# First expert tile turned inside the last projection, the last three gate tiles moved into the first up products

## What is computed

```python
x = x + xattn(layernorm(x), ctx, mask, Wq, Wk, Wv, Wo, bo)
h = layernorm(x)
scores = sigmoid(h @ gate.T + bias)                 # 9 experts
top, selected = top_k(scores, 2); top = top / (sum(top) + 1e-20)
for e in range(9):
    out += cw[:, e:e+1] * ((silu(h @ w1[e].T) * (h @ w3[e].T)) @ w2[e].T)
x = x + out
```

## Time and profile before

| | before |
|---|---|
| median of three runs | 441.45 us (439.77 to 442.72) |
| the profiled execution | 439.8 us, its span 438.0 us |
| TensorE busy | 408.5 us (93%) |
| VectorE, ScalarE, GpSimd busy | 294.6, 233.4, 253.1 us |
| mean granted clock of TensorE | 0.984 |

### The profile page before, as it was taken

One profiled execution on the slowest core, in us unless ns is written; L12 is line 12 of the kernel. 1 busy time (PEld: TensorE's weight loads), 2 busy tenths in 40 slices (PEclk: granted clock), 3 DMA queues, 4 the chain that ended last, 5 costly groups with the idle time before them and its releaser, 6 DMA issues.

```text
span 438.0 us, 10047 instructions
## 1 busy us (share of the span) xinstructions
PE 408.5 (93%) x3133; PEld 308.6 (70%) x3133; DVE 294.6 (67%) x719; ACT 233.4 (53%) x407; POOL 253.1 (58%) x187
## 2 busy tenths in 40 slices
PE   8799899999999999677999999999999999999981
PEld 8577577777777787564676777777777777777760
DVE  1868898999999999988879765444444444444320
ACT  3556697888788833406754443444444444444430
POOL 4504799998898974324126554555555555555242
PEclk9999999999999999988999999999999999999996
DMA  8963246766766425117886987999888899888782
GB/s 268 366 245 103 75 133 185 197 192 168 198 186 201 151 70 194 36 49 208 189 153 131 167 140 132 143 139 141 142 140 140 127 144 148 139 138 140 115 103 25
DMA packets 107408, 66.38 MB, mean 152 GB/s; under 512 B 82400, under 2 KB 100704, under 8 KB 107360
## 3 DMA queue, kind: packets, MB, share of 16 engines
q1 hardware_dynamic: 99680, 55.25, 54.1%
q0 software_dynamic: 7680, 10.49, 16.1%
HBM read 36.23 MB, written 9.96 MB: 105 GB/s over the span
## 4 chain that ended last, share of the span: by engine, by line
PE 75%; DVE 13%; DMA 3%; ACT 3%; issue 3%; POOLq 0%; DVEq 0%; POOL 0%; SPq 0%; ACTq 0%
PE ps L744 28%; PE ps L757 14%; PE ps L596 11%; PE ps L573 10%; PE ps L584 3%; PE ps L495 2%; PE ps L568 2%; DMA work<-work 2%; PE ps L534 1%; DVE w_all L1014 1%; DVE work L1059 1%; PE ps L542 1%; DVE work L1068 1%; DMA stage<-in_wt 1%; DMA work<-xn_rows,idx_all 1%
## 5 line engine op out<-in xcount | busy, mean ns | idle before, releaser
L744 PE MATMUL ps<-w_all,work 128*128 x960 | 151.6, 315 | 1.0 <-DVE w_all L1117 0.6
L744 PEld LDWEIGHTS ps<-w_all,work 128*128 128x128 f16 x960 | 94.1, 99 | 48.9 <-issue 1.7
L1546 POOL DMA_INDIRECT out_rows<-work,idx_all x40 | 63.3, 1584 | 94.4 <-ACT work L940 84.5
L1386 DVE SCALAR_TENSOR_TENSOR work<-ps,work 128x352 f32<-128x352 f32 x80 | 41.4, 523 | 67.9 <-PE ps L744 65.9
L757 PE MATMUL ps<-w_all,work 128*128 x680 | 80.8, 273 | 2.6 <-DMA work<-work 2.6
L757 PEld LDWEIGHTS ps<-w_all,work 128*128 128x128 f16 x680 | 66.1, 98 | 13.8 <-issue 3.5
L1525 POOL DMA_INDIRECT work<-xn_rows,idx_all x40 | 54.1, 1351 | 32.7 <-DVE work L1379 11.8
L1473 POOL TENSOR_TENSOR w_all<-stage,w_all 128x1088 f16<-128x1088 f32 x28 | 63.1, 2253 | 13.8 <-ACT w_all L827 13.8
L935 ACT ACTIVATE work<-work 128x704 f16<-128x704 f32 x40 | 31.6, 789 | 61.7 <-DVE work L1386 59.8
L929 ACT ACTIVATE work<-ps 128x352 f32<-128x352 f32 x80 | 36.2, 461 | 43.1 <-PE ps L744 42.6
L573 PE MATMUL ps<-w_all 128*128 128x462 f16 (+1 forms) x288 | 57.4, 336 | 0.0
(11 more groups left out here) (146 smaller groups left out, 542.7 us busy)
## 6 DMA issues: line engine op xcount, KB each, us to landing
stage<-in_wt SPq DMA_DIRECT2D x36, 544.0 KB, 4.4
work<-in_x SPq DMA_DIRECT2D x30, 128.0 KB, 3.7
out_rows<-work SPq DMA_DIRECT2D x18, 128.0 KB, 4.5
xn_rows<-work SPq DMA_DIRECT2D x18, 128.0 KB, 4.2
w_all<-in_x SPq DMA_DIRECT2D x1, 1536.0 KB, 14.2
work<-work SPq DMA_TRANSPOSE x79
w_all<-in_wk SPq DMA_DIRECT2D x2, 512.0 KB, 5.1
w_all<-in_wq SPq DMA_DIRECT2D x4, 256.0 KB, 6.7
```

The lines of the kernel that those rows point to most:

```text
L744: mm = pe.matmul(ps[:, c, 0:half], xt[:, t % 2, block, :], weights(wbase + off, half), start=(k == 0 and n == 0), stop=(k == KD - 1 and n ...
L1386: dve.scalar_tensor_tensor(out=sg[:, t % 2, cols], in0=ps[:, 2 + c, 0:HID // 2], scalar=1.0 / SP_W, in1=sg[:, t % 2, cols], op0=ALU.mult, ...
L1546: pool.indirect_dma_start(out=acc, out_offset=bass.IndirectOffsetOnAxis(ap=idx_all[:, t:t + 1], axis=0), in_=yb[:, t % 2], in_offset=None, ...
```

## The change

On **TensorE** the first expert tile is turned inside the last projection, ahead of chunk 7 (`X0_AT`). Only `gate_turn(13)` stays ahead of up(0); the logits of tiles 13, 14 and 15 go into the middle of up(0), up(1) and up(2), and `gate_turn(14)` and `gate_turn(15)` behind up(0) and up(1). The first expert id is read ahead of the last projection. On **ScalarE** the sigmoids come in two parts, for token tiles 0 to 10 in the drain and 11 to 15 at tile 3, and a one-element Silu stands ahead of `first_high`; so a table of functions is loaded at these places and again ahead of silu(4). On **VectorE** `first_low` comes ahead of the picks of tiles 11 and 12 and of w_rest(28); the residual and the normalisation of the last tiles go behind `fx_low(1)`, the logits of tile 13 behind w_rest(31), those of 14 and 15 into tiles 1 and 2. `shares` works on 11 tiles at tile 1 and on 5 at tile 5. **GpSimd** issues gather(2) ahead of `rstd(15)`, and **SyncE** turns tile 1's tokens ahead of two row stores.

```diff
-            def project(i):
+            def project(i, midway=None):
...
+                    if c == X0_AT and midway:
+                        midway()
...
                 warm(WARM_OUT, WARM_LATE)
-                project(NT - 1)
-                first_turn()
+                eids[0] = expert(0)
+                project(NT - 1, first_turn)
                 gate_turn(NT - 3)
-                gate_logits(NT - 3)
-                gate_turn(NT - 2)
-                gate_logits(NT - 2)
...
-            def next_expert(t):
-                if t < NF:
-                    eids[t] = expert(t)
+            def between(s):
+                if s < 3:
+                    gate_logits(NT - 3 + s)
+                if s + 1 < NF:
+                    eids[s + 1] = expert(s + 1)
...
-                if s == 0:
-                    gate_turn(NT - 1)
-                    gate_logits(NT - 1)
+                if s < 2:
+                    gate_turn(NT - 2 + s)
...
             gate_copy(NT + 1 - LAG_G)
+            sigmoids(0, K1)
             w_direct(4 * EARLY + 1)
+            w_direct(4 * EARLY + 2)
+            act.activation(mx[:, 0, 0:1], eps[:], ACT.Silu)
             first_high()
-            gate_copy(NT - 3)
-            w_direct(4 * EARLY + 2)
...
+                if n == 0:
+                    silu(n)
                 if onf(n, -2) and n > -2:
                     fx_high(n + 2)
                 if n == -1:
-                    gate_copy(NT - 2)
+                    gate_copy(NT - 3)
                     w_direct(4 * EARLY + 3)
...
-                if n == 1:
-                    sigmoids()
-                if onf(n, 0):
+                if onf(n, 0) and n > 0:
                     silu(n)
-                if n == 0:
-                    gate_copy(NT - 1)
+                if n in (0, 1):
+                    gate_copy(NT - 2 + n)
                 if n == 3:
+                    sigmoids(K1, NT)
...
                 held_of(0)
-                pick(NT - LAG_G)
                 normalise2(NT - 3)
                 logits(NT + 1 - LAG_G)
+                first_low()
+                pick(NT - LAG_G)
                 pick(NT + 1 - LAG_G)
                 w_rest(4 * EARLY)
-                residual(NT - 1)
-                first_low()
-                stats(NT - 1)
-                aggregate(NT - 1)
-                normalise2(NT - 2)
-                logits(NT - 3)
-                pick(NT - 3)
-                w_rest(4 * EARLY + 1)
...
                 if n == -1:
+                    residual(NT - 1)
+                    stats(NT - 1)
+                    aggregate(NT - 1)
+                    normalise2(NT - 2)
+                    w_rest(4 * EARLY + 1)
                     w_rest(4 * EARLY + 2)
                     normalise2(NT - 1)
-                    logits(NT - 2)
+                    w_rest(4 * EARLY + 3)
+                    logits(NT - 3)
+                    pick(NT - 3)
+                if n in (1, 2):
+                    logits(NT - 3 + n)
+                if n == 1:
                     pick(NT - 2)
-                    w_rest(4 * EARLY + 3)
...
                 if n == 2:
+                    pick(NT - 1)
+                    experts_of(1)
                     w_rest(4 * E9 - 4)
...
                 if n == 5:
+                    shares(1)
```

More of the change, by code:

```diff
@@ L344, in build @@
         WARM_BANK, WARM_LATE = 5, 2
+        X0_AT = 7
         B_CUTS = (0, 4, NCH)
@@ L448, in _ @@
             load_w(4 * EARLY + 3)
-            store_x1(NT - 1)
-            store_xn2(NT - 2)
             def turn_hidden(t):
@@ L475, in fstep @@
                 if n == -1:
+                    store_x1(NT - 1)
+                    store_xn2(NT - 2)
                     store_xn2(NT - 1)
@@ L692, in first_turn, with expert @@
                 mm.then_inc(x0_mm, 1)
+            def expert(t):
+                pe.wait_ge(eid_ok, 1 if t < NF1 else 2)
+                return pe.value_load(eid[0:1, t:t + 1], min_val=0, max_val=E9 - 1)
+            eids = {}
             def drain():
@@ L728, in weights, with up @@
                 return w_all[:, bass.ds(off, n)]
-            def up(t, wbase, after_gates):
+            def up(t, wbase, midway):
                 if t == 0:
@@ L747, in up @@
                     if c == 1:
-                        after_gates()
+                        midway()
             def down(t, wbase):
@@ L780, in _ @@
                         pe.wait_ge(w_lo_ok, 4 * E9)
-                    up(s, eids[s] * (2 * WC), lambda: next_expert(s + 1))
-                if s == 0:
-                    gate_turn(NT - 1)
-                    gate_logits(NT - 1)
+                    up(s, eids[s] * (2 * WC), lambda: between(s))
+                if s < 2:
+                    gate_turn(NT - 2 + s)
                 if s == 2:
@@ L853, in gate_copy, with sigmoids @@
                 act.activation(xn2t, ps[:, 7, 0:D].rearrange("p (k t) -> p k t", k=KD), ACT.Copy).then_inc(xn2t_ok, 1)
-            def sigmoids():
-                act.wait_ge(top_ok, NT)
-                act.activation(R["sgm"], top_val[:, 0:2 * NT].rearrange("p (i k) -> p k i", k=2), ACT.Sigmoid).then_inc(sig_ok, 1)
+            def sigmoids(i0, i1):
+                act.wait_ge(top_ok, i1)
+                act.activation(R["sgm"][:, :, i0:i1], top_val[:, 2 * i0:2 * i1].rearrange("p (i k) -> p k i", k=2),
+                               ACT.Sigmoid).then_inc(sig_ok, 1)
             def step(n):
@@ L1223, in held_of, with shares @@
                 dve.tensor_scalar(held[:, lo + 1:lo + n], r["ef"][:, 0:n - 1], 16.0, None, ALU.mult).then_inc(held_ok, 1)
[L1225 to L1234, removed]
+            def shares(ph):
+                lo, hi = (0, K1) if ph == 0 else (K1, NT)
+                sgm, cwv, v1, v2 = (a[:, :, lo:hi] for a in (r["sgm"], r["cwv"], r["val"][:, 0], r["val"][:, 1]))
+                wsum, wrec = r["wsum"][:, lo:hi], r["wrec"][:, lo:hi]
+                dve.wait_ge(sig_ok, ph + 1)
+                link(dve.tensor_tensor(wsum, sgm[:, 0], sgm[:, 1], ALU.add))
+                link(dve.tensor_scalar(wsum, wsum, 1e-20, None, ALU.add))
+                link(dve.reciprocal(wrec, wsum))
+                link(dve.tensor_tensor(cwv, sgm, wrec.unsqueeze(1).to_broadcast([P, 2, hi - lo]), ALU.mult))
+                link(dve.tensor_copy(v1, cwv))
+                link(dve.tensor_tensor(v2, cwv, v1, ALU.subtract))
             def tile_weights(ph):
@@ L1371, in first_shares @@
             def first_shares():
-                shares()
+                shares(0)
                 link(tile_value(r["u1"][:, :, :, 1, :], ueq1, 1, K1, NF1))
@@ L1412, in fstep @@
                     hidden(n)
-                if n == 0:
-                    logits(NT - 1)
-                    pick(NT - 1)
-                    experts_of(1)
                 if n == 1:
@@ L1563, in fstep @@
                     rstd(NT - 2)
-                    rstd(NT - 1)
                 if onf(n, -3):
                     gather(n + 3)
+                if n == -1:
+                    rstd(NT - 1)
             for n in range(F_FIRST, F_LAST):
```

## The result

The changed kernel takes 444.95 us (median of 4 runs, 444.55 to 446.68) beside 440.61 us (439.21 to 442.72) for the kernel before: ratio 1.009, interval 1.0056 to 1.0125. Its profiled execution has a span of 442.7 us against 438.0. The forecast of 442.8 had the sign and the places, but only a third of the size: +1.4 us was forecast, +4.3 came by the medians and +4.7 by the spans.

What follows compares the result with a forecast made beforehand. TensorE, busy 93% of the span, and its holes bound the kernel. +1.0 us at first_weights and +0.4 from silu(4) make +1.4: span 439.4, 441.2 like the profiled execution, forecast 442.8 from the median; range 440.0 to 446.0.

Steps and rivals of the forecast that it cites:

- the forecast's own mechanism: The forecast's chain of shifts at up(1), first_weights and up(5), together +1.4 us; chance 0.52, expected at 441.3 to 444.5.
- Start of up(0): TensorE behind the last projection: up(0) starts at about 197.4, 3.9 us earlier, and is over at 201.45.
- The new wait: TensorE ahead of gate_turn(14): stands 4.85 us for logits(13), behind w_rest(31) and its later load.
- Rival A: At gate_turn(14): logits(13) come in time and the front gain is kept; 437.7, or 436.5 without clock loss; chance 0.09.
- The clock: TensorE's clock falls again after the empty 4.85 us, now in up(1), costing 1.4 us, between nothing and 1.7.
- Rival B: Clock also falls ahead of up(5), 1.7 us more; load(31) up to 3.0 slower; both from 445.9 up; chance 0.13.
- Rival D: A wash: clock holds in up(1), only logits(15) delays first_weights, by 0.5 us; 442.0 or 441.5; chance 0.22.
- Start of up(1): On TensorE, up(1) starts at 206.55 instead of 207.87, 1.3 us earlier.
- the wait for logits(15): Ahead of first_weights: logits(15), moved to tile 2 on VectorE, end at 216.5; the wait adds 0.3 us.
- The table load: ScalarE, right ahead of silu(4): a 1.28 us load makes up(5) wait 1.1; down(4)'s old wait gives 0.7 back.
- rival C: On ScalarE: switching tables costs a drain on top of the load; 444.2 us; chance 0.04.
- shares(1): VectorE at tile 5: six small instructions, 1.4 us at most, covered by 1.9 us spare between h_low(5) and down(5).

Runs made afterwards that it cites:

- x10: The changed kernel itself, unchanged, timed and profiled a second time: ratio 1.0111 to the kernel before.
- x5: The changed kernel with w_rest(28) ahead of first_low on VectorE again: ratio 0.9998 to the kernel before.
- x6: The changed kernel with w_rest(28) ahead of first_low and the logits and pick of tile 13 ahead of w_rest(29): ratio 1.0018 to the kernel before.
- x3: The changed kernel with 70 matmuls on constants between up(0) and gate_turn(14): ratio 1.0118 to the kernel before.
- x4: The changed kernel with the logits and pick of tile 13 ahead of w_rest(29) to w_rest(31) on VectorE: ratio 1.0071 to the kernel before.
- x2: The changed kernel with a one-element Silu ahead of w_direct(35), loading the table in ScalarE's idle time: ratio 1.0077 to the kernel before.
- x8: x7 with w_rest(31) moved behind hidden(0) on VectorE: ratio 1.0036 to the kernel before.
- x9: x7 with fx_low(2) directly behind w_rest(29), and one load and turn_tokens(2) ahead of the last row store: 439.71 us, ratio 0.9959 to the kernel before.
- x1: The changed kernel with the second part of the shares at tile 6 instead of tile 5: ratio 1.0070 to the kernel before.
- x7: The changed kernel with the edits of x1, x2 and x6, and the picks of tiles 11 and 12 ahead of first_low: ratio 0.9973 to the kernel before.

## Why the prediction was right, and where it was off

**The range.** 444.95 lies within 440.0 to 446.0, but 0.45 above the 441.3 to 444.5 that were given for the forecast's own mechanism. And the median of before came out at 440.61, 0.84 below the 441.45 that 442.8 was built on: the miss in the difference, 2.9 us by the medians, shows as 2.15 in the time. That part of the hit is luck, and the terms below are measured as shifts.

**Start of up(0): right.** 197.4 forecast, 197.74 found; it is over at 201.85 (201.45). The projection with the turn inside ended 0.3 us later than assumed; reading the id ahead made the wait before the projection 0.27 us longer (it starts at 192.29, not 192.10; TensorE reads the id from 191.3 to 192.1, when p_low is there already, at 191.89). It had been costed at nothing.

**The new wait: right in mechanism, and in size in this execution.** 4.85 us forecast, 4.89 found, both ends 0.4 us later, over the chain as written, down to the load at 4.0 us. In the second profile (x10) the load took 5.1 and the hole was 6.0, so the exact match is partly luck. One thing was seen too lightly. The forecast named the load as what is late, at 0.5 us behind VectorE's other work. x5 shows that with the load early 2.9 us of hole remain: the logits were late by their place in VectorE's order anyway. Rival A, the logits in time, would have needed both edits at once, and x6 has them: up(1) at 203.75, 6.25 us after up(0), where A had 203.7 by the transposed tokens. So A had the next bound right, but not the end: it gave 437.7, and x6 is level with before, since up(2), up(5) and down(5) wait next. (The 436.5 beside it has no working.)

**The clock: right that it falls, wrong in size.** "It falls again, now in up(1), and costs 1.4 us, between nothing and the 1.7": up(1) took 6.66, 1.2 more than the forecast 5.45, and 2.7 more than the 3.95 of x3. The upper bound was a single case taken for a limit. Over seven such holes, in six kernels, from 2.9 to 6.0 us long, the cost was 1.1 to 2.7; 1.4 lay inside, 1.7 did not bound it. Of the missed 3.3 us, 1.2 is this term in the profiled execution. x10 lost only 1.7 there, so most of this part belongs to the execution, not to the kernel. Rival B expected a second fall at up(5), which came in no run, and a slower load(31), which came in part: 5.1 us in x4 and x10. Rival D had the clock hold; of the kernels with the hole at the gate turn only x3, with the hole filled, shows that, and its median gained nothing.

**Start of up(1): -0.68 for -1.3.** Logits and gate turn were some 0.4 us later than forecast (206.74 for 206.3), and the gate turn took 0.45 at the low clock where 0.25 was taken: 0.6 us. With the clock's 1.2 they are the 1.8 us by which up(2) missed its forecast (+2.03 for +0.2).

**first_weights: the wait for logits(15) was small.** Forecast +0.3 for it. The logits are over at 218.15 and first_weights starts at 218.21; up(2) took 4.14 us, where up(1) in x3, with nothing to wait for, took 3.95. So some 0.2 us of wait are left. The forecast had 4.05 for up(2) and 0.3 for the wait, 0.2 too much together.

**The table load: right.** Start of the load to the next ACTIVATE 1.29 us again (231.64, 232.93), TensorE's hole 1.13 for 1.1, and x2 takes it away. No drain beside it, the next instruction follows 0.01 us behind the load: rival C falls. The 0.64 us that down(4) waited before was given back, as forecast.

**shares(1): the step that failed.** "The spare 1.9 covers it" took 4.0 us for the transpose, from the earlier trace rows, which is that of the tile before. The transpose of tile 5 is this row of the chain of waits after:

```profile
243.97 5.62 DMA work<-work
```

5.62 us. SyncE's row of its issue in before is

```profile
239.43 1.31 SPq L456 DMA_TRANSPOSE work<-work  x1
```

and down(5) started at 245.18, 5.75 later, without a hole. If the transpose took as long there as after, nothing was spare, and not 1.9. How long it did take in before no row shows, only that it had landed within those 5.75 us. But tile 5's transpose was slower than tile 4's in every profile that shows it as a wait: 5.0 to 5.9 us (the change twice, x2 to x6), where tile 4's took 4.0 to 4.1 (before, x2, x8, x9). The price with the cover gone was given (1.4, found 1.5), and the cover was gone. This is 1.6 of the missed 3.3 us (from down(4) to down(5) 7.16 us, and 6.81 in x10, where before had 5.57), and x1 takes it back. So the trace of before held no proof of the slack: the 5.75 us leave some 1.8 spare only if this transpose, too, takes 4.0.

Together 1.2 for the clock, 0.6 for the start of up(1), 1.6 for shares, less 0.2 ahead of first_weights: 3.2 of 3.3.

What stays open: whether load(35) in x3 was slow by chance, why tile 5's transpose takes longer than tile 4's, and why a transpose of tile 1's tokens took at most 4.0 us in x8 and x9 and, as I read it, 5.7 in x7.

## What to carry to other kernels

Starting one tile earlier moves the wait to the next thing in an in-order queue, and each engine has to be put in order behind it: freeing a buffer late delays a load on one engine, a copy on the second and a product on the third. A transfer that ends in time shows no wait, so a trace gives only an upper bound of its duration, from its own issue to the start of its user; a duration borrowed from another tile does not prove slack, and a run with the edit elsewhere, as x1, tells whether it was there. An empty stretch of TensorE is priced as itself plus, where the clock falls, the slow product behind it, and both ends of that price need more than one sample.

## What the runs showed of the hardware

**What a hole costs afterwards.** Holes of 1.6 to 1.9 us (x6, x7, x9) and one of 2.78 (x3, ahead of up(5)) were followed by full speed. Behind longer ones the next product, 3.95 us at full clock, took longer by: 1.65 us after 2.90 (x5), 2.6 after 3.02 (x8, in up(2)), 2.35 after 4.58 (x4), 1.1 after 4.84 (x2), 2.7 after 4.89 (the change), 1.8 after 5.44 (x1), 1.7 after 6.00 (x10). The cost does not grow with the hole. Filled with 70 matmuls on constants (x3) the clock stayed at 1.00.

**The same transfer, different times.** load(31) reached its user 4.0, 5.1 and 5.1 us after issue (the change, x4, x10), load(35) 4.0 and 5.8 (the change, x3). The transposes of the hidden rows, all of one size, took 3.97 to 4.11 us for tile 4 (before, x2, x8, x9) and 4.96 to 5.87 for tile 5 (x2 to x6, and the change with 5.62 and 5.28).

**Table loads.** The load on ScalarE took 1.28 us, and the next ACTIVATE began 1.29 us after its start (after, 231.64 and 232.93; x2, 225.07 and 226.36), with no drain beside it. In ScalarE's idle time it cost TensorE nothing (x2).
